# Softmax sums of the first query half from the masked first scores

## The chip, the cores and the metric

The kernel runs on one core of a Trainium2 chip. The metric is the device time of one execution in microseconds. Below, TensorE, VectorE, ScalarE, GpSimd and SyncE are the engines that the profile calls PE (PEld for its weight loads), DVE, ACT, POOL and SP.

## The reference

Two layers over x of shape 4 x 1024 x 512. Layer 0 is a causal softmax attention (16 heads of 32) with a projection, a residual and a layer norm, then a feed-forward part with ternary weights; layer 1 is a linear attention and a second feed-forward part. The change touches only this:

```
q, k, v = (x @ w).reshape(B, S, H, hd).transpose(0, 2, 1, 3)     # each
scores = einsum('bhqd,bhkd->bhqk', q, k) / sqrt(hd)
scores = where(causal, scores, finfo.min)
attn = softmax(scores, axis=-1)
ctx = einsum('bhqk,bhkd->bhqd', attn, v)
```

## The kernel before, in words

Layer 0's attention works in 16 units (`NU`), each a batch element and a group of four heads (`HPG`). A unit has 1024 queries in two halves of 512 (`CH`), c = 0 and c = 1, and 8 blocks of 128 keys.

Scores are computed twice. The first time (`score_entry`, L971) queries lie on partitions; VectorE adds the causal mask and takes the row maximum in one instruction (`reduce_rows`, L191), whose full output goes to a scrap buffer, `junk`. A half has 16 such tiles: `SHORT` for c = 0, with 128, 256, 384 or 512 keys, `LONG` for c = 1, with 640 to 1024 in two PSUM banks. After a half's last tile the maxima are negated and split into a high and a low part (L195, L198), turned by TensorE (`turn`, L202), copied (L1112) and written by two DMAs (`load_max`, L183) as two more rows of the queries. The second time (`scores_T`, L984) keys lie on partitions, and the two more rows subtract the maximum, so that ScalarE only has to take exp (L1080) into `probs`. GpSimd clears the masked corner of diagonal blocks (L871). TensorE multiplies `probs` with v (`with_v`, L1000, into `O_BANK`) and, for the softmax sums, with a block of ones (`with_ones`, L1011, into `SUM_BANK`). At the end of a half ScalarE copies `O_BANK` (`evacuate`, L1072), and VectorE normalizes in four parts: a transpose of the sums (L1142), a reciprocal (L1145), a transpose back (L1148), a multiplication (L1154). SyncE stores the half (L893).

A unit has ten steps (`STEPS`), three for the first half and seven for the second. The order of TensorE's work is written out as a string for each step: `s` is the scores of one head for this step, `e` the next entry of the *next* unit's first scores, `v` and `o` the products with v and with ones of the step *before*. The entries (`ROUND`, 34 of them) are the 16 short tiles with the turned rows of c = 1 at place 5, then the 16 long ones with the turned rows of c = 0 behind the fifth. The steps hold 9, 3, 3, 3, 3, 3, 2, 4, 2 and 2 entries. Scores of both kinds take the PSUM banks 0 to 5 as a ring: TensorE waits for whoever used a bank before. v of step 3 waits for the copy of the first half (`o_read`), since both halves use one `O_BANK`. ScalarE's instructions stand in one order: the exponentials of step n + 1, then, behind step 3 and behind the next step 0, the copy of a half. The last unit has no entries but one.

The first stage (`phase_qkv0`) computes q, k and v; in its last batch it holds the first scores of unit 0 (L399, `ENTRIES`, `PLACES`), one or two of them between outputs, which ScalarE copies (L503, L507).

Elsewhere in the kernel, `L1410` counts with ScalarE's Square and `accum_out`, `L1423` and `L1100` are plain ScalarE copies in SBUF, and `L1995` has a bias that is a column of SBUF.

Of the kernel before, what the change touches and what calls it, by code (L numbers as in the profile page):

```python
# [26 lines left out]
P = 128  # L27
# [5 lines left out]
CH = 512  # L33
# [120 lines left out]
class Scores:  # L154


    kst: object
# [7 lines left out]
    bound: object  # L165

# [18 lines left out]
    def reduce_rows(self, dve, bank, junk, c, tile, g):  # L185
# [8 lines left out]
    def negate_hi(self, dve, c):  # L194
        return dve.tensor_scalar(self.negmax[:, c, 0, :], self.rowmax[:, c, :], -1.0, None, ALU.mult)  # L195

    def negate_lo(self, dve, c):
        return dve.scalar_tensor_tensor(out=self.negmax[:, c, 1, :], in0=self.rowmax[:, c, :], scalar=-1.0,  # L198
                                        in1=f32(self.negmax[:, c, 0, :]), op0=ALU.mult, op1=ALU.subtract)
# [5 lines left out]
def phase_qkv0(nc, program, psum, ident, x_t, wq, wk, wv, q_dram, k_dram, v_dram, ffn_w, first, qk_stored, v_stored):  # L205
# [12 lines left out]
    with Phase(program) as ctx:  # L218
# [37 lines left out]
        rm_done, nm_ready, max_loaded = sem("p1_rm_done"), sem("p1_nm_ready"), sem("p1_max_loaded")  # L256
        x_v = x_t.rearrange("b (k p) (c t) -> b c p k t", p=P, c=2)
# [6 lines left out]
        TURN = PER_UNIT + 5  # L264
# [15 lines left out]
        with nc.Block() as block:  # L280
# [199 lines left out]
            def _(act):  # L480
                act.sem_inc(v_copied, 4)

# [13 lines left out]
                def body(b, last):  # L496
                    for c in range(2):
                        for o in range(OUTS):
# [9 lines left out]
                            if 4 <= o < 4 + KT and not (c and last):  # L508
                                x_hi(b + c, 1 - c, o - 4)
                batches(act, body)  # L510

            @block.vector
            def _(dve):
# [22 lines left out]
                def maximum(k):  # L536
# [9 lines left out]
                    if c == 1:  # L546
                        dve.wait_ge(s_used, k + 1)
                    elif k >= 4 and k % 2 == 0:
                        dve.wait_ge(s_used, k)
                    to = first.junk[:, k % 2, k % 4 // 2 * CH:] if c == 0 else first.junk[:, k % 2, :]  # L550
                    first.reduce_rows(dve, bank_of(k), to, c, tile, g).then_inc(s_used, 1)
                    if (tile, g) == (CT - 1, HPG - 1):
                        dve.wait_ge(s_used, 2 + k + 1)
                        first.negate_hi(dve, c).then_inc(rm_done, 1)
                        dve.wait_ge(rm_done, c + 1)
                        first.negate_lo(dve, c).then_inc(nm_ready, 1)
# [72 lines left out]
def phase_attention(nc, program, psum, ident, q_dram, k_dram, v_dram, o_dram, ffn_w, first, qkv_stored, tern, kept, tmp, after, ahead):  # L629
# [14 lines left out]
    STEPS = [([(0, 0)], "seseeseeeeseevo"), ([(0, 1), (0, 3)], "sesessevo"),  # L644
             ([(0, 2)], "eeesssvos"), ([(1, 0)], "esesssevo"),
# [4 lines left out]
    HALF_ENDS = [3, N_STEPS]  # L650
    ST_PER_UNIT = HPG * N_STEPS
# [14 lines left out]
    with Phase(program, ahead) as ctx:  # L666
# [40 lines left out]
        sum_read = sem("p2_sum_read", 1)  # L707
        rec_step = sem("p2_rec_step")
# [9 lines left out]
        bias_stage = first.causal[:, 0:D]  # L718
# [1888 lines left out]
```

## Time and profile before

| | us |
|---|---|
| median of 3 runs | 2439.05 (2438.56 to 2439.28) |
| profiled execution | 2436.57 |
| its span | 2435.0 |
| TensorE busy | 2372.1 (97%) |
| VectorE busy | 1214.1 (50%) |
| ScalarE busy | 824.4 (34%) |
| GpSimd busy | 862.6 (35%) |

The span runs from the first to the last instruction of the profile; the 1.6 us beside it lie outside. Busy shares are of the whole span, in which the layer-0 attention is one of six stages, and shares of a stage are read from its own slices and windows. TensorE's instructions are pipelined: the start times of its rows tell how long a group took, and the durations of neighbours overlap. ScalarE's overlap too, so a row that merges n instructions has a duration of n - 1 distances and one last instruction.

### The profile page before, as it was taken

The page shows a single profiled execution, that of the slowest core. Times are in us where ns is not written, and L with a number is a line of the kernel's source. Part 1 is how long each engine was busy: PE and PEld are TensorE (multiplying, and loading weights), DVE is VectorE, ACT ScalarE, POOL GpSimd, SP SyncE. Part 2 cuts the span into 40 slices and gives each one's busy share as a digit, 9 for nine tenths or more (in the row PEclk, how much of TensorE's full clock was granted, in tenths as well). Part 3 has the DMA queues.
Part 4 walks back from the last instruction along what each step waited for, and adds up shares of the span by engine and source line. Part 5 has one row for each costly group of instructions (what it writes and reads, how often), then busy time and mean ns, then how long its engine had stood idle before and what let it go on. Part 6 is the DMA issues. An engine that isn't in the chain of part 4 may idle for free. (4 is left out here: it accounts for less than half of the span.)

```text
span 2435.0 us, 39858 instructions
## 1 busy us (share of the span) xinstructions
PE 2372.1 (97%) x12749; PEld 1783.5 (73%) x12749; DVE 1214.1 (50%) x2551; ACT 824.4 (34%) x1392; POOL 862.6 (35%) x1098
## 2 busy tenths in 40 slices
PE   9999999999999999999999996999999999999997
PEld 7887755555555557788888885888888888888886
DVE  4334577777777758422222207776764732222221
ACT  3222355555555543344444431011111222222221
POOL 2000256565665552233333334442425221222112
PEclk9999999999999999999999998999999999999999
DMA  8895354545445328512121104140404242222200
GB/s 285 282 300 183 109 131 111 142 119 124 118 119 137 100 86 295 139 35 52 34 52 34 40 30 160 36 172 21 152 34 153 89 109 53 52 52 52 58 29 35
DMA packets 265860, 262.55 MB, mean 108 GB/s; under 512 B 128051, under 2 KB 161843, under 8 KB 265269
## 3 DMA queue, kind: packets, MB, share of 16 engines
q1 hardware_dynamic: 250148, 218.44, 31.2%
q0 software_dynamic: 6128, 24.21, 3.2%
q10 hardware_dynamic: 9504, 18.88, 2.3%
q8 instruction: 46, 0.75, 0.1%
q14 instruction: 34, 0.27, 0.0%
HBM read 168.68 MB, written 92.27 MB: 107 GB/s over the span
## 5 line engine op out<-in xcount | busy, mean ns | idle before, releaser
L191 DVE CUSTOM_DVE_ANT_0 junk<-psum,causal 128x896 bf16<-128x896 f32 (+7 forms) x512 | 373.3, 751 | 163.2 <-PE psum L971 137.8
L1080 ACT ACTIVATE p_probs<-psum 128x512 f32<-128x512 f32 (+1 forms) x640 | 317.4, 555 | 269.0 <-PE psum L984 264.8
L1607 POOL TENSOR_TENSOR p_h_lo<-p_h,p_h_hi 128x512 fp32r<-128x512 f32 x128 | 164.3, 1284 | 303.5 <-ACT p_h_hi L1630 303.5
L984 PE MATMUL psum<-qst,kst 98*128 98x512 f32 (+3 forms) x768 | 220.8, 367 | 1.8 <-PEq L280 0.9
L871 POOL TENSOR_SCALAR_AFFINE_SELECT p_probs<-p_probs 128x128 f32<-128x128 f32 x512 | 140.7, 297 | 223.3 <-ACT p_probs L1080 221.0
L2394 ACT ACTIVATE p_h<-psum,ffn_b 128x512 f16<-128x512 f32 x128 | 88.0, 688 | 372.5 <-PE psum L1259 357.6
L2370 POOL CAST p_h<-p_h 128x512 fp32r<-128x512 f16 x128 | 85.0, 664 | 364.6 <-ACT p_h L2394 364.1
L971 PE MATMUL psum<-kst,qst 96*128 96x128 f32 (+3 forms) x720 | 207.7, 362 | 0.8 <-ACT p_probs L1080 0.8
L984 PEld LDWEIGHTS psum<-qst,kst 98*128 98x128 f32 x768 | 130.8, 189 | 106.1 <-DVE rowmax L191 42.7
L1656 PE MATMUL psum<-tern,p_h_hi 128*128 128x512 f32 x512 | 199.4, 390 | 2.5 <-POOL p_h_lo L1607 2.5
L1656 PE MATMUL psum<-tern,p_h_lo 128*128 128x512 f32 x512 | 199.3, 389 | 0.0
L1622 ACT ACTIVATE p_h<-psum,ffn_b,alpha 128x512 f32<-128x512 f32 x128 | 99.8, 780 | 260.6 <-PE psum L1259 256.7
L971 PEld LDWEIGHTS psum<-kst,qst 96*128 96x128 f32 x720 | 123.6, 189 | 69.5 <-DVE rowmax L191 42.6
L2474 DVE TENSOR_TENSOR ffn_rows<-psum,p_b 128x512 f16<-128x512 f32 x32 | 19.9, 683 | 280.5 <-PE psum L2418 280.5
L1000 PE MATMUL psum<-p_probs,v 128*32 128x512 f32 (+3 forms) x1536 | 157.0, 496 | 1.9 <-ACT p_probs L1080 1.1
L1011 PE MATMUL psum<-p_probs,p_ones 128*32 128x512 f32 (+3 forms) x1536 | 154.4, 489 | 0.0
L1259 PE MATMUL psum<-ffn_xT,la_w_hi 128*128 128x512 f32 x384 | 149.6, 389 | 1.2 <-PEq L1859 1.2
L2418 PE MATMUL psum<-p_w_hi,p_h 128*128 128x512 f32 x384 | 149.5, 389 | 0.0
L2418 PE MATMUL psum<-p_w_lo,p_h 128*128 128x512 f32 x384 | 149.4, 389 | 0.0
L1259 PE MATMUL psum<-ffn_xT,la_w_lo 128*128 128x512 f32 x384 | 149.4, 389 | 0.0
L1656 PEld LDWEIGHTS psum<-tern,p_h_hi 128*128 128x128 f32 x512 | 96.1, 188 | 23.2 <-issue 1.8
L1656 PEld LDWEIGHTS psum<-tern,p_h_lo 128*128 128x128 f32 x512 | 96.0, 188 | 19.9
(260 smaller groups left out, 4902.5 us busy)
## 6 DMA issues: line engine op xcount, KB each, us to landing
qst<-q_parts SPq DMA_DIRECT2D x96, 256.0 KB, 4.8
kst<-k_parts SPq DMA_DIRECT2D x96, 256.0 KB, 6.8
q_parts<-p_qk_out SPq DMA_DIRECT2D x32, 512.0 KB, 3.7
k_parts<-p_qk_out SPq DMA_DIRECT2D x32, 512.0 KB, 3.4
v_rows<-p_v_out SPq DMA_DIRECT2D x32, 256.0 KB, 4.4
v<-v_rows SPq DMA_DIRECT2D x16, 512.0 KB, 4.1
attention_out<-p_o_out SPq DMA_DIRECT2D x32, 256.0 KB, 2.1
p_x<-in_x SPq DMA_DIRECT2D x8, 1024.0 KB, 6.7
```

What stands on the lines that cost most here:

```text
L191: return dve.tensor_tensor_reduce(view(junk[:, 0:n]), bank, view(self.causal[:, SEQ - n:SEQ]), 1.0, FLOOR, ALU.add, ALU.max, self.rowmax[: ...
L871: pool.affine_select(out=blk, in_=blk, compare_op=ALU.is_ge, fill=0.0, base=0, pattern=[[1, P]], channel_multiplier=-1).then_inc(p_masked, 1)
L971: mm = pe.matmul(psum[:, bank, 0:keys], qst[slot][0:KD, c, g, tile * P:(tile + 1) * P], kst[slot][0:KD, g, k0:k0 + keys], start=True, stop ...
L984: mm = pe.matmul(psum[:, bank, col:col + CH - q0], kst[s][0:KD + 2, g, j * P:(j + 1) * P], qst[s][0:KD + 2, c, g, q0:CH], start=True, stop ...
L1000: mm = pe.matmul(O_BANK[g * HD:(g + 1) * HD, q0:CH], vs[s][:, j, g * HD:(g + 1) * HD], probs[:, n % 2, g, col:col + CH - q0], start=(n == ...
L1011: mm = pe.matmul(SUM_BANK[g * HD:(g + 1) * HD, q0:CH], ones[:, :], probs[:, n % 2, g, col:col + CH - q0], start=(n == half_at), stop=(n + ...
L1080: act.activation(probs[:, n % 2, g, col:CH], psum[:, banks_of(s, "s", st)[0], col:CH], ACT.Exp, scale=SM_SCALE).then_inc(p_ready, 1)
L1259: mm = pe.matmul(bank, lhsT, rhs, start=(n == 0), stop=(n == len(terms) - 1))
L1607: pool.tensor_tensor(h_lo[:, m % 2, :], h[:, m % 2, :], f32(h_hi[:, m % 2, :]), ALU.subtract).then_inc(hl_done, 1)
L1622: H.free(act.activation(h[:, t % 2, :], H.bank(m), ACT.Gelu, bias=b1c[:, t:t + 1], scale=alpha[:, 0:1]), m)
L1656: mm = pe.matmul(Y.bank(m), src[:, t % 2, tok], tern2[:, t, :], start=(t == 0 and part == 0), stop=(t == HT - 1 and part == 1))
L2418: mm = pe.matmul(Y.bank(m), h[:, t % 2, a * P:(a + 1) * P], w(t), start=(t == 0 and part == 0), stop=(t == HT - 1 and part == 1))
```

## The change

The softmax sums of the first half no longer come from products with ones. VectorE's instruction for a short tile now writes the masked scores, times minus the scale, as f32 to one of three slots of `junk`, and takes their minimum. ScalarE then takes exp of the slot in place with the row's extreme as bias and the row sum as accumulated output (`sum_row`), two entries behind (`SUM_BEHIND`), between its exponentials of the unit in work (`work`). After the sixteenth sum it takes the logarithm and exp of its negative (`logarithms`); VectorE corrects the logarithm with these and subtracts it from the maximum (`fold`), behind the fifth long tile (`FOLD`), and only then splits the shift. The probabilities of the first half are so already normalized: the products with ones, and VectorE's normalization, are dropped for it, and ScalarE copies `O_BANK` straight to the output buffer. The strings of steps 1 to 3 lose their `o`. The rows of c = 0 are turned behind the eighth long tile instead of the fifth. VectorE waits for the sum of three tiles before when it reuses a slot. ScalarE's wait for the buffer of probabilities is for the products with v where there are none with ones. The causal mask becomes bf16. In the first stage the 16 sums of unit 0 stand between ScalarE's copies of the last batch, and a preload of the table set natural_log_exp_and_others is issued at its start.

```diff
+        if c == 0:
+            return dve.tensor_tensor_reduce(junk[:, 0:n], bank, self.causal[:, SEQ - n:SEQ], -SM_SCALE, -FLOOR,
+                                            ALU.add, ALU.min, self.rowmax[:, c, col:col + 1])
...
+    def sum_row(self, act, n, tile, g):
+
+        scores, col = self.slot(n)[:, 0:P * (tile + 1)], g * CT + tile
+        return act.activation(scores, scores, ACT.Exp, bias=self.rowmax[:, 0, col:col + 1], scale=-1.0,
+                              accum_out=self.sums[:, 0, col:col + 1])
+
+    def logarithms(self, act, log_done, inverse_done, value):
+
+        act.activation(self.sums[:, 1, :], self.sums[:, 0, :], ACT.Ln).then_inc(log_done, 1)
+        act.wait_ge(log_done, value)
+        act.activation(self.sums[:, 2, :], self.sums[:, 1, :], ACT.Exp, scale=-1.0).then_inc(inverse_done, 1)
...
+        dve.tensor_tensor(self.sums[:, 3, :], self.sums[:, 0, :], self.sums[:, 2, :], ALU.mult).then_inc(ratio_done, 1)
+        dve.wait_ge(ratio_done, value)
+        dve.scalar_tensor_tensor(out=self.sums[:, 2, :], in0=self.sums[:, 3, :], scalar=-1.0, in1=self.sums[:, 1, :],
+                                 op0=ALU.add, op1=ALU.add).then_inc(log_better, 1)
+        dve.wait_ge(log_better, value)
+        dve.scalar_tensor_tensor(out=self.sums[:, 4, :], in0=self.sums[:, 2, :], scalar=-1.0, in1=self.rowmax[:, 0, :],
+                                 op0=ALU.mult, op1=ALU.add).then_inc(folded, 1)
...
-        TURN = PER_UNIT + 5
+        FOLD, TURN = PER_UNIT + 4, PER_UNIT + 8
...
-    STEPS = [([(0, 0)], "seseeseeeeseevo"), ([(0, 1), (0, 3)], "sesessevo"),
-             ([(0, 2)], "eeesssvos"), ([(1, 0)], "esesssevo"),
+    STEPS = [([(0, 0)], "seseeseeeeseevo"), ([(0, 1), (0, 3)], "sesessev"),
+             ([(0, 2)], "eeesssvs"), ([(1, 0)], "esesssev"),
...
+        FOLD, LONG_BEHIND = LONG[4], 8
+        ROUND = SHORT[:BEHIND] + [(0, 1, None, None)] + SHORT[BEHIND:] + LONG[:LONG_BEHIND] + [(1, 0, None, None)] + LONG[LONG_BEHIND:]
...
-                    if n == half_at:
-                        pe.wait_ge(sum_read, 2 * u + blocks_of(n)[0][0] + 1)
+                    if n == HALF_ENDS[0]:
+                        pe.wait_ge(sum_read, u + 1)
...
-                    act.wait_ge(o_normed, 1 + 2 * u + c)
-                    act.activation(o_raw[:, :], O_BANK, ACT.Copy).then_inc(o_read, 1)
+                    if c == 0:
+                        act.wait_ge(o_stored[0], 1 + 16 * u)
+                        act.activation(o_out[:, 0, :], O_BANK, ACT.Copy).then_inc(o_read, 1)
...
+                def row_sum(u, k):
+                    if k < 0 or ROUND[k] not in SHORT:
+                        return
+                    _, _, tile, g = ROUND[k]
+                    n = SHORT.index(ROUND[k])
+                    if n == 0:
+                        act.wait_ge(folded, 1 + u)
+                    act.wait_ge(s_used, S_RING + PER_ROUND * u + k + 1)
+                    first.sum_row(act, n, tile, g).then_inc(sum_done, SUMMED_TO[n + 1] - SUMMED_TO[n])
+                    if n == PER_UNIT - 1:
+                        act.wait_ge(sum_done, PER_ROUND * u + SUMMED_TO[-1])
+                        first.logarithms(act, log_done, inverse_done, 1 + u + 1)
+                        act.sem_inc(sum_done, PER_ROUND - SUMMED_TO[-1])
+
+                def work(u, s, n, end=False):
+
+                    wait_probs(u, n)
+                    head, k = 0, ENTRY_AT[n]
+                    for what in STEPS[n][1]:
+                        if what == "s":
+                            exponential(u, s, n, head)
+                            head += 1
+                        elif what == "e":
+                            if not end:
+                                row_sum(u, k - SUM_BEHIND)
+                            k += 1
...
-                        to = first.junk[:, (n + 2) % 4 // 2, n % 2 * CH:]
-                        alone = n % 2 == 0
+                        to = first.slot(n)
+                        if n >= 3:
+                            dve.wait_ge(sum_done, at + 1)
...
+                    if e == FOLD:
+                        dve.wait_ge(inverse_done, 1 + u + 1)
+                        first.fold(dve, ratio_done, log_better, folded, 1 + u + 1)
+                        dve.wait_ge(folded, 1 + u + 1)
+                        shift(unit, 0)
...
+                           far("junk", [P, 3, SEQ], BF16), far("rowmax", [P, 2, HPG * CT], F32), far("negmax", [P, 2, 2, HPG * CT], F32R),
+                           far("max_rows", [2 * HPG * CT, 2, P], F32), far("causal", [P, SEQ], BF16), far("bound", [P, 2, 3], F32),
+                           far("sums", [P, 5, HPG * CT], F32))
```

## Rows read from the trace of the kernel before

**Rows 1.** the page, 40 slices of the span (60.9 us each), busy tenths.

```profile
ACT  3222355555555543344444431011111222222221
...
PEclk9999999999999999999999998999999999999999
```

**Rows 2.** grouped lines, 285 to 896 us; busy, mean ns, idle before and releasers.

```profile
L191 DVE CUSTOM_DVE_ANT_0 junk<-psum,causal 128x128 bf16<-128x128 f32 (+3 forms) x480 | 349.0, 750 | 143.5 <-PE psum L971 137.8 <-issue 2.8 <-DVE rowmax L191 0.3
...
L1011 PE MATMUL psum<-p_probs,p_ones 128*32 128x512 f32 (+3 forms) x1536 | 154.4, 489 | 0.0
```

**Rows 3.** windows, steps 0-3 and 4-9: length, busy PE, PEld, DVE, ACT, POOL (x instructions), clock.

```profile
554.58:568.17 13.59, 13.52 (x124) 8.23 (x120) 10.79 (x44) 8.41 (x18) 6.19 (x17) 1.00 0.68 169
568.17:593.01 24.84, 24.84 (x175) 12.12 (x171) 18.75 (x36) 12.62 (x25) 16.33 (x24) 1.00 0.40 99
```

**Rows 4.** timeline of TensorE: start, duration, line, tiles, count.

```profile
554.58 0.50 PE L984 MATMUL psum<-qst,kst 98*128 98x512 f32 x1
...
560.11 1.07 PE L1000 MATMUL psum<-p_probs,v 128*32 128x512 f32 x8
...
561.97 0.90 PE L971 MATMUL psum<-kst,qst 96*128 96x384 f32 x3
...
563.16 1.07 PE L1000 MATMUL psum<-p_probs,v 128*32 128x384 f32 x16
...
565.02 0.39 PE L984 MATMUL psum<-qst,kst 98*128 98x256 f32 x1
...
567.17 0.64 PE L1000 MATMUL psum<-p_probs,v 128*32 128x256 f32 x8
...
568.17 0.74 PE L984 MATMUL psum<-qst,kst 98*128 98x512 f32 x2
...
569.36 1.06 PE L1000 MATMUL psum<-p_probs,v 128*32 128x512 f32 x8
570.36 0.56 PE L971 MATMUL psum<-kst,qst 96*128 96x320 f32 x2
...
573.27 1.06 PE L1000 MATMUL psum<-p_probs,v 128*32 128x512 f32 x8
...
593.04 0.51 PE L984 MATMUL psum<-qst,kst 98*128 98x512 f32 x1
```

**Rows 5.** timeline of ScalarE in the same unit.

```profile
555.12 1.58 ACT L1080 ACTIVATE p_probs<-psum 128x512 f32<-128x512 f32 x3 [2.23 <-PE psum L984]
...
558.01 0.60 ACT L1072 ACTIVATE p_o_raw<-psum 128x512 f32<-128x512 f32 x1 [0.32 <-PE psum L1000]
558.76 2.07 ACT L1080 ACTIVATE p_probs<-psum 128x512 f32<-128x512 f32 x4 [0.16 <-PE psum L984]
563.03 0.94 ACT L1080 ACTIVATE p_probs<-psum 128x256 f32<-128x256 f32 x3 [2.20 <-PE psum L984]
```

**Rows 6.** timeline of ScalarE elsewhere.

```profile
895.91 2.18 ACT L1100 ACTIVATE kst<-pieces 128x512 fp32r<-128x512 f32 x4
...
958.95 1.92 ACT L1423 ACTIVATE qst<-p_o 128x2048 fp32r<-128x2048 f32 x1 [9.86 <-PE psum L1259]
960.78 1.90 ACT L1410 ACTIVATE p_squares<-tern 128x2048 f16<-128x2048 f32 x1
962.57 0.19 ACT L1410 ACTIVATION_READ_ACCUMULATOR p_squares<-tern 128x1 f32 x1
962.79 1.92 ACT L1410 ACTIVATE p_squares<-tern 128x2048 f16<-128x2048 f32 x1
...
1498.41 2.42 ACT L1995 ACTIVATE p_qT<-psum,p_bq 128x512 f32<-128x512 f32 x4 [7.28 <-issue]
```

**Rows 7.** grouped lines of VectorE, 285 to 896 us.

```profile
L1154 DVE TENSOR_TENSOR p_o_out<-p_o_raw,p_recip 128x512 f32<-128x512 f32 x31 | 40.8, 1317 | 0.1
```

**Rows 8.** timeline of ScalarE in the first stage.

```profile
222.88 0.60 ACT L503 ACTIVATE p_qk_out<-psum 128x512 fp32r<-128x512 f32 x1 [1.94 <-PE psum L457]
```

**Rows 9.** grouped lines of ScalarE, whole span; one of three such rows.

```profile
L1435 ACT ACT_TABLE_LOAD x1 | 1.3, 1283 | 0.0
```

More of the change, by code:

```diff
@@ L165 @@
     bound: object
+    sums: object
     def load_qk(self, eng, q_dram, k_dram, u, s, c, r, of_q, loaded):
@@ L480, in _, with row_sums @@
             def _(act):
+                act.preload_act_table_set("natural_log_exp_and_others")
                 act.sem_inc(v_copied, 4)
+                def row_sums(entries):
+                    for k in entries:
+                        if k < PER_UNIT:
+                            act.wait_ge(s_used, 2 + k + 1)
+                            first.sum_row(act, k, *ENTRIES[k][1:]).then_inc(sum_done, 1)
+                        if k == PER_UNIT - 1:
+                            act.wait_ge(sum_done, PER_UNIT)
+                            first.logarithms(act, log_done, inverse_done, 1)
                 def x_hi(b, c, k, at_start=False):
@@ L509, in body @@
                                 x_hi(b + c, 1 - c, o - 4)
+                            if last and c == 0:
+                                row_sums(PLACES[0][o])
                 batches(act, body)
@@ L794, in phase_attention @@
         PARTS = 4
-        AFTER = [HALF_ENDS[c] % N_STEPS for c in range(2)]
-        FROM = [ENTRY_AT[n] + entries_in(STEPS[n][1].split("o")[0]) for n in AFTER]
-        TO = [FROM[c] + PARTS - 1 for c in range(2)]
-        assert TO[1] < FROM[0] and turned(1) < FROM[1]
+        FROM = entries_in(STEPS[0][1].split("o")[0])
+        TO = FROM + PARTS - 1
+        assert turned(1) < FROM and TO < PER_ROUND
+        SUM_BEHIND = 2
+        SUMMED_TO = [0] + [ROUND.index(e) + 1 for e in (SHORT + LONG)[3:PER_UNIT + 3]]
         def half(eng, body):
@@ L1085, in _ @@
                     act.wait_ge(stored, value)
-                exponentials(0, 0, 0)
+                work(0, 0, 0)
                 def body(i, last):
@@ L1091, in body @@
                         if n + 1 < len(steps):
-                            exponentials(*steps[n + 1])
+                            work(*steps[n + 1], last and steps[n + 1][1] == 1)
                         if step + 1 in HALF_ENDS:
@@ L1159, in entries, with normalize_between @@
                         maximum(at, banks_of(s, "e", k), ROUND[k], u)
[L1161 removed]
+                def normalize_between(u, around, s, first):
                     for part in range(PARTS):
[L1164 removed]
+                        normalize(u, part)
                         if part < PARTS - 1:
@@ L1192, in body @@
                         if last and s == 1:
-                            for part in range(PARTS):
-                                normalize(u, 0, part)
                             split_projection()
                             for part in range(PARTS):
-                                normalize(u, 1, part)
+                                normalize(u, part)
                             return
-                        entries(u, s, TO[1], FROM[0])
-                        normalize_between(u, 0, u, s, FROM[0])
-                        entries(u, s, TO[0], PER_ROUND)
+                        entries(u, s, TO, PER_ROUND)
                         if last:
```

131 lines of the change are left out of this document (81 added, 50 removed).

## The prediction

> **What bounds the kernel now.** I read the slices of the page first: the attention stage runs from about 285 to 895 us, TensorE at its full granted level, ScalarE at five to six tenths [rows 1]. Second come the grouped lines of that stage: the products with ones cost 154.4 us of TensorE there, beside VectorE's masked maxima with 349.0 us [rows 2]. Third, two stretches of one unit: in steps 0 to 3 (13.59 us) TensorE is busy 13.52, VectorE 10.79 and ScalarE 8.41 us; in steps 4 to 9 (24.84 us) TensorE is busy for all 24.84, ScalarE for 12.62 [rows 3]. A busy TensorE need not be a bound one, so the fourth view is its timeline: one unit's first matmul starts at 554.58, the next one's at 593.04, 38.46 us later, and in between the groups start behind one another with no idle time named [rows 4]. So the attention stage is 16 units of 38.4 us, set by TensorE's own order. ScalarE follows it: its exponentials start 0.54 us after the unit's first matmul and then wait for scores [rows 5]. The question for this change is which engine needs longer in each stretch, not over the stage: the new work on ScalarE lies almost wholly in steps 0 to 3.
>
> **What is removed from TensorE.** With ones behind, v and ones of step 0 take 560.11 to 561.97, 1.86 us, and those of step 1 563.16 to 565.02, 1.86 us; a v group with no ones behind takes 569.36 to 570.36, 1.00 us. That is 0.86 us less, twice. Step 2 (256 columns) takes 1.00 us with ones; in the same proportion 0.46 us go. Together 2.18 us a unit [rows 4]. For 16 units this would be 34.9 us, if TensorE stayed the bound.
>
> **What is added to ScalarE.** Every unit but the last prepares the next one's 16 short tiles, so 15 units have 16 sums each, four of each width 128, 256, 384, 512. The order puts sum n at the second entry behind its own. Counting the letters e of the steps: step 0 has 9 entries and so sums 0 to 5 (entry 5 is the turned rows), step 1 sums 6 to 8, step 2 sums 9 to 11, step 3 sums 12 to 14, step 4 sum 15 and the logarithms. ScalarE works in order, and the copy of the first half's output stands behind step 3, so 15 sums lie ahead of it. TensorE cannot start v of step 3 before that copy (with_v waits for o_read).
>
> The price of one sum. Plain instructions behind one another start 0.49 us apart at 512 columns (558.76: four end after 2.07, the last takes 0.60) and 0.28 at 256 [rows 5]. From SBUF, as here, four of 512 end after 2.18 us, 0.52 apart, and one of 2048 is followed after 1.83 us (958.95 to 960.78) [rows 6]. On the line through these, 128, 256, 384 and 512 columns take 0.19, 0.30, 0.41 and 0.52 us. To this comes the accumulator's read: instructions with one start 2.01 us apart (960.78 to 962.79) at 2048 columns, 0.18 more than the plain one. And the sum has its bias in a column of SBUF: four such of 512 columns end after 2.42 us (last 0.69), 0.58 apart, 0.09 more than 0.49 [rows 6]. So 0.27 on each: 0.46, 0.57, 0.68 and 0.79 us. Fifteen of them: 4 x (0.46 + 0.57 + 0.68) + 3 x 0.79 = 9.21 us, 0.61 each.
>
> ScalarE's demand from its first exponential to the end of the copy: 12 exponentials of 512 at 0.49 and 4 of 256 at 0.28, 7.00 us; the copy of the former unit's second half, 0.75 to the next instruction (558.01 to 558.76) [rows 5]; the sums, 9.21; the copy itself, 0.60. That is 17.56, and with the start at 0.54 the copy ends 18.10 us into the unit. In the kernel before v of step 3 starts at 569.36, 14.78 us into the unit [rows 4]. TensorE alone would be there at 14.78 - 2.18 = 12.6. So ScalarE becomes the bound of steps 0 to 3, and v of step 3 is 3.3 us later than before.
>
> Bounds of this term. Below: if the column's 0.09 lies under the instruction before, 15 x 0.09 = 1.35 less, +2.0. Above: ScalarE's first exponential of a step waits twice, for the probabilities' buffer and the scores; a copy with such a pair behind it is followed after 0.75 instead of 0.49, so up to 0.15 for each of four steps, and 0.1 to reach TensorE: +4.0. I take +3.5, as some of such waits will show on an engine that never idles.
>
> **Whether it is caught up.** From v of step 3 on, TensorE had 593.04 - 569.36 = 23.68 us with no idle time [rows 4], so a delay is kept. ScalarE has 3.91 us until v of step 4 (573.27): four exponentials 1.96, sum 15 with 0.79, and two tiny instructions with waits of their own for the logarithm, some 0.8 us by estimate. 3.55 fits, barely; a few tenths may show and lie in the range. From step 5 on ScalarE is half idle.
>
> **The other parts.** VectorE waits for a sum three tiles back before it reuses a slot, with later maxima and the turned rows queued behind, and TensorE's bank ring behind those. Its 10.79 us of steps 0 to 3 fit in 18, and sum n - 3 precedes in ScalarE's order, so this is ScalarE's pace again and is not counted twice. The half's normalization (two transposes, a reciprocal, a multiplication of 1.3 us) goes from VectorE [rows 7]; TensorE did not wait for it, so nothing is gained. Fold and shift add five operations of 16 columns there, beside it. The reductions read a bf16 mask and write f32: with one f32 source in PSUM I expect the same 750 ns mean; 10% either way, some 0.7 us on the 16 short ones, is covered while ScalarE sets the pace. The rows turned for the first half come three entries later, in step 6, and are needed in the next step 0, over 10 us later. The store waits for the copy instead of VectorE and leaves sooner; SP's later loads move with the unit. In the first stage 16 sums fall between outputs where ScalarE idles 1.94 us [rows 8], two sums (1.0 to 1.4 us) each: nothing. The last unit has no sums and saves up to 2.18 us, but its first steps already wait elsewhere; I take 1.
>
> **Sum.** 15 x 3.5 - 1 = +51.5 us. The profiled execution took 2436.57 us (span 2435.0); with it 2488. The median of the runs is 2.5 us above it: 2490.5, so 2490.
>
> **Rivals.**
> 1. The accumulator and the bias column cost nothing in a stream of short instructions, so that sums run at the plain pitch. For it: VectorE's own accumulator reads hide well. Against: ScalarE's read stands in its rows with time of its own between instructions [rows 6]. Then 15 sums take 5.16 us, v of step 3 starts at 14.05, 0.73 earlier: 15 x 0.73 + 2 = 13 us faster, 2426. It decides from a mean price of 0.61 - 3.3 / 15 = 0.39 us a sum down. Chance 0.12.
> 2. TensorE stays the bound, all 34.9 us come: 2404. That needs 15 sums in 3.7 us, 0.25 each, less than a plain 256 [rows 5], or waits that let TensorE go past them; the ring of six banks and the copy behind step 3 forbid it. Chance 0.05.
> 3. Half-way: part of the 0.27 hides, and the copies overlap better: 0 to +28 us, 2439 to 2467. Chance 0.13, of which 0.05 within 0.2%.
> 4. Two table loads a unit, one for Ln and one back, or waits on own results much longer than counted. In the trace of before a load takes 1.28 us, three in all [rows 9], since Exp and Copy need no change. 2 x 1.28 x 15 = 38 more, 2528 with full effect; partial effects end at 2500 to 2515. The preload added at the start speaks against. Chance 0.10.
> By the Trainium skill, "ScalarE: Activation LUTs", section "Table sets: the hidden batching unit", one set (natural_log_exp_and_others) holds exp and ln, so no load is needed between them; no row of before has an Ln to show it. By that rule rival 4 comes only from the waits; the chance above is already low by the preload alone.
>
> **Chances.** The forecast, ScalarE bound in steps 0 to 3: 0.60, own range 2467 (15 x 2.0 - 2) to 2498 (15 x 4.0 - 1). About 0.2%, 5 us, is what a measurement can tell from no change. Faster: 0.12 + 0.05 = 0.17. Same 0.05. Slower 0.60 + 0.08 + 0.10 = 0.78. The range goes from rival 1 (2426) to a part of rival 4 (2515).
>
> **What would show it.** In the profile after: units of about 42 us; TensorE idle ahead of scores and v groups of steps 0 to 3, released by ScalarE or by VectorE that waited for ScalarE's sums; ScalarE without gaps there, and sums 0.46 to 0.79 us apart; steps 4 to 9 as before; v groups of the first half 1.00 us to the next. Were units at 36.3 us, rival 2 holds; if sums take 0.4 us or less, rival 1; if table loads stand in the attention stage, rival 4.

## The result and the profile after

The changed kernel takes 2490.12 us (median of 4 runs, 2488.42 to 2498.07), the kernel before beside it 2439.16 (4 runs, 2438.56 to 2439.55): ratio 1.0218, interval 1.0205 to 1.0231, 51 us slower. The forecast was 2490. The profiled execution took 2488.42 us, with a span of 2486.7. The total came out as forecast, but two of its steps did not, and they nearly cancel: ScalarE costs less than I put, and the later half of each unit, which I put at nothing, costs as much again.

Line numbers below are those of each run's own kernel. In the changed one L1048 is the first scores, L1061 the second scores, L1077 the products with v, L1087 those with ones, L197 and L199 VectorE's reductions of short and long tiles, L209 the sums, L1164 the exponentials, L1149 and L1152 the copies of the first and second half and L945 GpSimd's mask; in the experiments they move by a few lines.

The page of the changed kernel, engines and three slice rows, answers to [rows 1]:

```profile
PE 2375.3 (96%) x12237; PEld 1770.9 (71%) x12237; DVE 1175.1 (47%) x2535; ACT 955.5 (38%) x1936; POOL 868.6 (35%) x1098
...
PE   9999999999999999999999997999999999999997
...
ACT  3223467676767662444444442010111212222221
...
PEclk9999999999999999999999998999999999999999
```

ScalarE stands at six to seven tenths in the attention stage, not five to six. That average names no bound, for TensorE still has nines there. Grouped lines, 285 to 955 us (busy, mean ns of one, idle before and who ended it), answer to [rows 2]:

```profile
L199 DVE CUSTOM_DVE_ANT_0 junk<-psum,causal 128x640 bf16<-128x640 f32 (+3 forms) x240 | 239.6, 1023 | 166.6 <-PE psum L1048 119.3 <-ACT junk L209 42.4 <-PE psum L242 3.8
...
L1048 PE MATMUL psum<-kst,qst 96*128 96x128 f32 (+3 forms) x720 | 221.1, 375 | 28.4 <-DVE rowmax L199 13.5 <-ACT p_probs L1164 13.3
L1077 PE MATMUL psum<-p_probs,v 128*32 128x512 f32 (+3 forms) x1536 | 157.9, 498 | 18.2 <-POOL p_probs L945 10.8 <-ACT p_o_out L1149 7.3
...
L209 ACT ACTIVATE junk<-junk,rowmax 128x128 f32<-128x128 f32 (+3 forms) x240 | 138.2, 587 | 0.4 <-PE psum L1077 0.4
...
L1087 PE MATMUL psum<-p_probs,p_ones 128*32 128x512 f32 (+3 forms) x1024 | 111.1, 517 | 0.0
L209 ACT ACTIVATION_READ_ACCUMULATOR junk<-junk,rowmax 128x1 f32 x240 | 54.1, 225 | 0.0
```

The ones cost 111.1 us instead of 154.4 [rows 2]: they did go. In their place TensorE idles: 28.4 us before score tiles and 18.2 before v groups, where the kernel before had 0.8 and 1.9. ScalarE is named for 13.3 + 7.3, GpSimd for 10.8 (its masks follow ScalarE's exponentials, so this is ScalarE again), and VectorE's long tiles for 13.5. That last one was not in the forecast.

One unit in two stretches, steps 0 to 3 and 4 to 9 (length; busy PE, PEld, DVE, ACT, POOL; clock; DMA), answers to [rows 3]:

```profile
579.60:594.11 14.51, 12.74 (x91) 7.25 (x87) 10.41 (x42) 13.97 (x44) 6.93 (x17) 1.00 0.64 158
594.11:621.85 27.74, 26.01 (x175) 12.01 (x171) 16.74 (x38) 15.21 (x33) 15.88 (x24) 1.00 0.34 89
```

The first stretch is 0.92 us longer than before, with ScalarE busy 13.97 of 14.51 us; the second 2.90 longer, although ScalarE is busy for little more than half of it. Part of that second figure is steps 0 to 3 still arriving late (the v of step 3 falls in it). TensorE's timeline of this unit (start, duration, line, tiles, [idle before <- releaser]) divides it, and answers to [rows 4] (units come in two lengths, 42.25 and 41.5 us in turn; this is one of the longer):

```profile
579.60 0.50 PE L1061 MATMUL psum<-qst,kst 98*128 98x512 f32 x1
...
585.72 0.44 PE L1048 MATMUL psum<-kst,qst 96*128 96x384 f32 x1 [0.40 <-ACT p_probs L1164]
...
589.31 1.07 PE L1077 MATMUL psum<-p_probs,v 128*32 128x384 f32 x16 [0.65 <-POOL p_probs L945]
...
592.81 0.80 PE L1048 MATMUL psum<-kst,qst 96*128 96x320 f32 x2 [0.54 <-ACT p_probs L1164]
...
596.16 1.06 PE L1077 MATMUL psum<-p_probs,v 128*32 128x512 f32 x8 [0.40 <-ACT p_o_out L1149]
...
602.89 0.62 PE L1048 MATMUL psum<-kst,qst 96*128 96x384 f32 x2 [0.64 <-DVE rowmax L199]
...
610.61 0.47 PE L1048 MATMUL psum<-kst,qst 96*128 96x448 f32 x1 [0.59 <-DVE rowmax L199]
...
621.85 0.50 PE L1061 MATMUL psum<-qst,kst 98*128 98x512 f32 x1
```

The v of step 3 starts 16.56 us into the unit, released by the copy, against 14.78 before: 1.8 us later, not 3.3. From it to the next unit TensorE needs 25.69 us instead of 23.68 [rows 4]: 2.0 more in this unit, with two waits for long tiles in it. ScalarE over the first of these parts, answers to [rows 5]:

```profile
580.14 1.08 ACT L1164 ACTIVATE p_probs<-psum 128x512 f32<-128x512 f32 x2 [2.23 <-PE psum L1061]
581.11 0.40 ACT L209 ACTIVATE junk<-junk,rowmax 128x128 f32<-128x128 f32 x1
581.40 0.20 ACT L209 ACTIVATION_READ_ACCUMULATOR junk<-junk,rowmax 128x1 f32 x1
581.49 0.60 ACT L1164 ACTIVATE p_probs<-psum 128x512 f32<-128x512 f32 x1
...
584.59 0.59 ACT L1152 ACTIVATE p_o_raw<-psum 128x512 f32<-128x512 f32 x1
585.06 0.60 ACT L1164 ACTIVATE p_probs<-psum 128x512 f32<-128x512 f32 x1
...
595.43 0.68 ACT L1149 ACTIVATE p_o_out<-psum 128x512 f32<-128x512 f32 x1
...
597.82 0.22 ACT L214 ACTIVATE sums<-sums 128x16 f32<-128x16 f32 x1
598.07 0.22 ACT L216 ACTIVATE sums<-sums 128x16 f32<-128x16 f32 x1
598.23 1.09 ACT L1164 ACTIVATE p_probs<-psum 128x512 f32<-128x512 f32 x2
```

No idle time is named between 580.14 and the copy. Over the stage, a sum is followed by the next instruction after 0.384, 0.491, 0.598 and 0.706 us (medians of 60 each, from start to start, by width 128 to 512). Fifteen are 4 x (0.384 + 0.491 + 0.598) + 3 x 0.706 = 8.0 us. No table load stands around the logarithm. VectorE in step 5:

```profile
597.96 0.82 DVE L199 CUSTOM_DVE_ANT_0 junk<-psum,causal 128x640 bf16<-128x640 f32 x1 [1.33 <-ACT junk L209]
...
602.75 0.20 DVE L220 TENSOR_TENSOR sums<-sums 128x16 f32<-128x16 f32 x1
602.98 0.17 DVE L222 SCALAR_TENSOR_TENSOR sums<-sums 128x16 f32<-128x16 f32 x1
...
603.61 0.17 DVE L238 SCALAR_TENSOR_TENSOR negmax<-sums,negmax 128x16 fp32r<-128x16 f32 x1
603.86 0.96 DVE L199 CUSTOM_DVE_ANT_0 junk<-psum,causal 128x768 bf16<-128x768 f32 x1
```

The five operations of fold and shift take 1.1 us, from 602.75 to 603.86, and stand between two long tiles. TensorE's wait of 0.64 us at 602.89 above is for the long tile ahead of them, whose reduction ends as they start. What they cost shows a little later; in the unit before this one:

```profile
563.48 0.73 PE L1061 MATMUL psum<-qst,kst 98*128 98x512 f32 x2 [0.43 <-DVE rowmax L199]
```

There TensorE waits for the long tile that stands behind the fold.

The table that the rest goes by: the time from the first matmul of each v group to that of the next, taken from the matmul records of each trace, medians over 14 units in us (mean of even and odd units where they differ; kernels named by their experiments below).

```
                     9>0   0>1   1>2   2>3  | 3>4   4>5   5>6   6>7   7>8   8>9 | unit
before               2.89  3.05  4.01  2.20 | 3.90  5.34  3.56  5.51  3.47  4.51 | 38.43
changed              3.52  3.21  4.04  2.81 | 3.90  6.48  4.04  5.56  3.46  4.84 | 41.86
1 one column         2.89  2.19  3.35  1.77 | 3.90  8.36  4.91  5.55  3.46  4.55 | 40.92
2 no accumulator     3.23  3.09  3.53  2.63 | 3.90  6.75  4.04  5.56  3.46  4.75 | 40.94
3 long tiles to PSUM 3.52  3.21  4.04  2.82 | 3.92  6.56  4.07  5.56  3.47  4.84 | 42.01
4 unused ones        3.52  3.21  4.45  2.82 | 3.90  6.47  4.03  5.55  3.46  4.84 | 42.25
5 fold earlier       3.52  3.21  4.04  2.81 | 3.90  8.85  4.23  5.55  3.46  4.84 | 44.42
6 fold later         3.52  3.21  4.04  2.82 | 3.90  6.47  3.76  5.14  3.46  4.84 | 41.16
7 column, fold later 2.89  2.19  3.35  1.77 | 3.90  6.47  3.76  5.14  3.46  4.55 | 37.48
8 spread             2.76  4.33  3.54  1.65 | 3.83  5.34  3.93  8.18  5.85  4.83 | 44.45
```

The change costs 3.43 us a unit (forecast 3.5): 1.43 in the first four columns and 0.33 in the last, which is ScalarE; 1.67 in columns 4>5 to 6>7, which is something else. Of these 1.67, 4>5 grows by 1.1 us in every unit, but 5>6 only in every second one (4.51 us; 3.57 in the others, as before).

The granted clock differs between these traces. From 300 us to the stage's last v group it was 1.00 throughout in the kernel before, the changed one and experiments 2, 4 and 7. It was at the lower level (0.50, 1.2 GHz) for 3 us in experiment 6, 7 in 3, 41 in 1, 58 in 5 and 61 in 8. In experiment 1 a unit with 6.8 us of it takes 42.0 us, a unit of the same kind without it 39.0. So a microsecond at the lower level costs some 0.44 us (3.0 / 6.8), which makes 18, 25 and 27 us in experiments 1, 5 and 8, by estimate. Their rows of the table hold this too.

### The profile page after: what moved, and what is told of

It is laid out like the page before. It is cut to its first block and busy times, and to the rows that moved or that the text cites. A ratio compares the mean times of both kernels' runs of the same rounds, so it can differ in the third digit from the quotient of the medians.

```text
span 2486.7 us, 39530 instructions
## 1 busy us (share of the span) xinstructions
PE 2375.3 (96%) x12237; PEld 1770.9 (71%) x12237; DVE 1175.1 (47%) x2535; ACT 955.5 (38%) x1936; POOL 868.6 (35%) x1098
## 5 line engine op out<-in xcount | busy, mean ns | idle before, releaser
L1164 ACT ACTIVATE p_probs<-psum 128x512 f32<-128x512 f32 (+1 forms) x640 | 324.4, 567 | 201.0 <-PE psum L1061 199.4
L199 DVE CUSTOM_DVE_ANT_0 junk<-psum,causal 128x640 bf16<-128x640 f32 (+3 forms) x256 | 256.0, 1023 | 177.1 <-PE psum L1048 119.3
L1048 PE MATMUL psum<-kst,qst 96*128 96x128 f32 (+3 forms) x720 | 221.1, 375 | 28.4 <-DVE rowmax L199 13.5
L945 POOL TENSOR_SCALAR_AFFINE_SELECT p_probs<-p_probs 128x128 f32<-128x128 f32 x512 | 148.6, 312 | 269.2 <-ACT p_probs L1164 267.1
L1061 PE MATMUL psum<-qst,kst 98*128 98x512 f32 (+3 forms) x768 | 227.3, 373 | 5.9 <-DVE rowmax L199 3.5
L1061 PEld LDWEIGHTS psum<-qst,kst 98*128 98x128 f32 x768 | 132.9, 190 | 116.7 <-ACT p_probs L1164 43.6
L1048 PEld LDWEIGHTS psum<-kst,qst 96*128 96x128 f32 x720 | 124.3, 190 | 119.3 <-ACT p_probs L1164 51.8
L1077 PE MATMUL psum<-p_probs,v 128*32 128x512 f32 (+3 forms) x1536 | 157.9, 498 | 18.2 <-POOL p_probs L945 10.8
L197 DVE CUSTOM_DVE_ANT_0 junk<-psum,causal 128x128 f32<-128x128 f32 (+3 forms) x256 | 121.5, 486 | 73.8 <-issue 32.4
L209 ACT ACTIVATE junk<-junk,rowmax 128x128 f32<-128x128 f32 (+3 forms) x256 | 147.0, 584 | 0.4 <-PE psum L1077 0.4
```

What stands on the lines that cost most here:

```text
L197: return dve.tensor_tensor_reduce(junk[:, 0:n], bank, self.causal[:, SEQ - n:SEQ], -SM_SCALE, -FLOOR, ALU.add, ALU.min, self.rowmax[:, c, ...
L209: return act.activation(scores, scores, ACT.Exp, bias=self.rowmax[:, 0, col:col + 1], scale=-1.0, accum_out=self.sums[:, 0, col:col + 1])
L945: pool.affine_select(out=blk, in_=blk, compare_op=ALU.is_ge, fill=0.0, base=0, pattern=[[1, P]], channel_multiplier=-1).then_inc(p_masked, 1)
L1048: mm = pe.matmul(psum[:, bank, 0:keys], qst[slot][0:KD, c, g, tile * P:(tile + 1) * P], kst[slot][0:KD, g, k0:k0 + keys], start=True, stop ...
L1061: mm = pe.matmul(psum[:, bank, col:col + CH - q0], kst[s][0:KD + 2, g, j * P:(j + 1) * P], qst[s][0:KD + 2, c, g, q0:CH], start=True, stop ...
L1077: mm = pe.matmul(O_BANK[g * HD:(g + 1) * HD, q0:CH], vs[s][:, j, g * HD:(g + 1) * HD], probs[:, n % 2, g, col:col + CH - q0], start=(n == ...
```

## The experiments

Eight kernels, each run beside the kernel before; its median was 2438.61 beside experiments 1 to 4, 2438.26 beside 5 and 2437.55 beside 6 to 8.

### 1. The sums nearly taken away

```diff
-        return act.activation(scores, scores, ACT.Exp, bias=self.rowmax[:, 0, col:col + 1], scale=-1.0,
-                              accum_out=self.sums[:, 0, col:col + 1])
+        return act.activation(self.sums[:, 0, col:col + 1], scores[:, 0:1], ACT.Exp, scale=-1.0)
```

> The kernel after, but a sum reads one column of its slot instead of 128 to 512, without bias and accumulator; its waits, slots and places stay. (Sums are not computed.) Theory, ScalarE's time in steps 0 to 3 sets the unit: 15 such instructions take some 0.2 us each, 3.0 instead of 8.0, so TensorE's own order is the bound again, units near 36.3 us and the time 2404 to 2412. Rival, the hand-over VectorE to ScalarE and back through three slots sets the pace whatever a sum costs: units stay above 39 us, 2450 or more.

Measured 2473.24 (2469.55 to 2476.11), ratio 1.0141 (1.0124 to 1.0158): neither. In the table steps 0 to 3 are at TensorE's pace (first four columns: 10.20, in the changed kernel 13.58), so that half of the theory holds. What was won there is lost in 4>5 and 5>6. Its timeline, three engines mixed:

```profile
628.51 2.36 POOL L911 TENSOR_TENSOR pieces<-pieces,tern 128x1024 f32<-128x1024 f32 x1 [0.18 <-POOL tern L908]
...
629.17 1.73 DVE L219 TENSOR_TENSOR sums<-sums 128x16 f32<-128x16 f32 x1
...
632.83 1.22 PE L1060 MATMUL psum<-qst,kst 98*128 98x512 f32 x2 [1.91 <-DVE rowmax L199]
...
635.69 1.94 PE L1076 MATMUL psum<-p_probs,v 128*32 128x512 f32 x8
```

and the window right behind the wait, columns as above:

```profile
632.85:639.50 6.65, 6.65 (x24) 2.65 (x25) 1.96 (x5) 2.17 (x4) 0.00 (x0) 0.51 0.34 111
```

The reader is to see two things. VectorE's first fold operation, 16 columns wide, takes 1.73 us instead of 0.20: it ends at 630.90, where GpSimd's product of two tiles in SBUF ends (628.51 + 2.36 = 630.87). Over the stage the fifteen of them have a mean of 1.51 us. And after the wait of 1.91 us TensorE ran at a granted clock of 0.51, its 1.2 GHz level: the v group takes 1.94 us instead of 1.07. By the estimate above this lower level is some 18 us of the run. The Trainium skill has the rule for the first, "SBUF — State Buffer", section "SBUF: two separate sides": VectorE and GpSimd share a pair of ports, held by one of them for a whole instruction, and a VectorE operation with two inputs in SBUF needs it against a GpSimd operation that reads SBUF. This trace agrees. In this kernel the fold falls inside GpSimd's product; in the changed kernel ScalarE makes it late enough to fall into the product's last 0.3 us at most.

### 2. The sums without their accumulator

```diff
-        return act.activation(scores, scores, ACT.Exp, bias=self.rowmax[:, 0, col:col + 1], scale=-1.0,
-                              accum_out=self.sums[:, 0, col:col + 1])
+        return act.activation(scores, scores, ACT.Exp, bias=self.rowmax[:, 0, col:col + 1], scale=-1.0)
```

> The kernel after, but the exponentials of the sums have no accumulated output (256 reads fewer; the sums are a constant). Theory: a sum is dearer than a plain exponential by the accumulator's read, 0.18 us each. Fifteen of them in steps 0 to 3 give back 2.7 us a unit, 40 us in all, and VectorE is less late behind them: 2435 to 2450. Rival, the read hides under the next instruction and the price is the columns': 2485 to 2490.

Measured 2475.55 (2474.15 to 2478.03), ratio 1.0153 (1.0136 to 1.0170), between the theory and its rival. The pitches are now 0.292, 0.400, 0.506 and 0.614 us, 0.092 less each (0.091 at 256). So the read costs 0.092 us in a stream of short instructions, half of the 0.18 that I took from instructions of 2048 columns [rows 6]. Without it they stand within 0.02 of the line of the prediction plus its 0.09 for the bias column (0.28, 0.39, 0.50, 0.61): those terms were right. Per unit 1.10 + 0.09 us are won in the first four columns and 8>9, and 0.27 given back in 4>5. There the fold's first operation comes earlier, towards GpSimd's product:

```profile
L219 DVE TENSOR_TENSOR sums<-sums 128x16 f32<-128x16 f32 x15 | 7.5, 500 | 0.0
```

Its mean is 500 ns against 238 (3.6 us for 15) in the changed kernel, 0.26 more a unit.

### 3. No waits of the long tiles for the sums

```diff
+        out = bank if junk is None else view(junk[:, 0:n])
-        return dve.tensor_tensor_reduce(view(junk[:, 0:n]), bank, ...
+        return dve.tensor_tensor_reduce(out, bank, ...
...
-                        n = LONG.index((1, c, tile, g))
-                        to = first.junk[:, n % 3, :]
-                        if n < 3:
-                            dve.wait_ge(sum_done, at + 1)
-                        elif n % 2 == 1:
-                            dve.wait_ge(s_used, S_RING - 2 + at + 1)
+                        to = None
```

> The kernel after, but the long tiles' full output goes back to their own PSUM banks, so VectorE needs no slot for them and waits for no sum there. Theory: 1.9 us of a unit's 3.4 us loss lie behind v of step 3, and most of it is VectorE, which waits for sums 14 and 15 before long tiles 1 and 2 (1.1 and 1.3 us in the trace after) and is late for TensorE's bank ring in steps 5 to 7: 1.2 to 1.6 us a unit come back, 2466 to 2473. Rival, those late steps come from the fold's chain of five operations or from ScalarE itself: 2485 to 2491. Should PSUM output be slow, the long tiles' mean (1023 ns) shows it.

Measured 2500.80 (2492.95 to 2503.85), ratio 1.0259 (1.0242 to 1.0276): the theory fell. The profiled execution is the fastest of the four, with a mean granted clock of 0.992; the others had 0.985 to 0.988, so part of the median is clock that the table doesn't show. VectorE's 42.4 us of waits for `junk` are gone, and no column of the table is shorter. A named wait of 1.1 to 1.3 us, some tiles ahead of the place that hurts, was slack. The long tiles cost a little more each than with 1023 and 83 ns; the rest of the 0.15 us a unit is not explained:

```profile
L200 DVE CUSTOM_DVE_ANT_0 psum<-psum,causal 128x640 f32<-128x640 f32 (+3 forms) x240 | 243.7, 1043 | 162.8 <-PE psum L1049 158.6 <-PE psum L243 2.9
...
L200 DVE DVE_READ_ACCUMULATOR2_ANT rowmax<- 128x1 f32 x240 | 33.9, 141 | 0.0
```

### 4. The ones put back, unused

```diff
-    STEPS = [([(0, 0)], "seseeseeeeseevo"), ([(0, 1), (0, 3)], "sesessev"),
-             ([(0, 2)], "eeesssvs"), ([(1, 0)], "esesssev"),
+    STEPS = [([(0, 0)], "seseeseeeeseevo"), ([(0, 1), (0, 3)], "sesessevp"),
+             ([(0, 2)], "eeesssvps"), ([(1, 0)], "esesssevp"),
...
+                        elif behind and what == "p":
+                            unused_ones(*behind)
```

> The kernel after with the first half's products with ones put back at their old places, their result unused: TensorE gets its 2.18 us a unit again. Theory: in steps 0 to 3 TensorE waits for ScalarE, 16.6 us against 12.6 of its own, so the products lie in that wait: 2490 to 2500. Rival, TensorE's work still counts in full there: 15 to 16 times 2.18, 2523.

Measured 2495.35 (2495.19 to 2496.63), ratio 1.0234 (1.0217 to 1.0251), as expected. Products that the kernel before paid with 2.18 us a unit cost 0.39 here, all of it in 1>2. So in steps 0 to 3 TensorE is not the bound of the changed kernel, and removing them brought next to nothing.

### 5. The fold one long tile earlier

```diff
-        FOLD, LONG_BEHIND = LONG[4], 8
+        FOLD, LONG_BEHIND = LONG[3], 8
```

> The kernel after with FOLD = LONG[3] instead of LONG[4]: nothing else moves. The e3 run did not give back the loss behind v of step 3, so that part of the theory fell. New theory: it is VectorE's chain of five small operations (1.1 us) put between long tiles 4 and 5, exactly when TensorE's ring asks for their banks; behind long tile 3 VectorE idles 2.3 us, and the chain is free there. v of step 4 to v of step 6 (10.5 us against 8.9 before) comes back to 9.0 to 9.3, 1.2 to 1.5 us a unit: 2467 to 2473. Rival, the delay behind v of step 3 is ScalarE's order or the later turn of the rows: 2487 to 2492.

Measured 2529.29 (2527.48 to 2535.18), ratio 1.0380 (1.0360 to 1.0400): 39 us slower than the changed kernel, where I expected a gain; the rival's 2487 to 2492 did not come either. Its timeline:

```profile
617.83 0.94 DVE L220 TENSOR_TENSOR sums<-sums 128x16 f32<-128x16 f32 x1
...
618.92 2.38 POOL L912 TENSOR_TENSOR more<-more,tern 128x1024 f32<-128x1024 f32 x1 [0.18 <-POOL tern L909]
619.01 2.32 DVE L225 SCALAR_TENSOR_TENSOR sums<-sums,rowmax 128x16 f32<-128x16 f32 x1
...
622.84 0.62 PE L1048 MATMUL psum<-kst,qst 96*128 96x384 f32 x2 [2.21 <-DVE rowmax L199]
```

GpSimd's product (618.92 + 2.38 = 621.30) starts 0.09 us ahead of VectorE's operation, and VectorE's ends at 621.33. The fold's first operation, with 0.94 us, ended in the same way with the operation that GpSimd did before (616.35 to 618.73, a difference of two tiles). A reduction, whose scores are in PSUM, ran inside that one without growing: 0.82 us at 617.09, as at 597.96 above.

Column 4>5 rises by 2.37 us, and the wait is the smaller part of it. In the six units that keep the full clock it is 7.55 us, 1.1 more than in the changed kernel; in every second unit it is 10.1, and there the clock is low:

```profile
577.00:583.80 6.80, 6.28 (x21) 2.75 (x25) 3.47 (x9) 2.02 (x4) 0.55 (x1) 0.50 0.23 77
```

So of the 39 us some 25 are the lower level's, by the estimate under the table.

### 6 and 7. The fold and the turned rows later

```diff
-        FOLD, LONG_BEHIND = LONG[4], 8
+        FOLD, LONG_BEHIND = LONG[7], 11
...
-                        if not end:
+                        if last and not end:
                             load_max(1 - s, 0, PER_ROUND * u + turned(0))
...
                                 load(u + 2, s, c)
+                                if c == 0:
+                                    load_max(1 - s, 0, PER_ROUND * u + turned(0))
```

> The kernel after with the fold behind long tile 7 (was 4), the rows of the first half turned behind long tile 10 (was 7), and on SyncE their load behind the next queries' loads instead of ahead of them. The run with the fold one tile earlier showed why it must not stand in GpSimd's stretch: there two small operations with both sources in SBUF ended only with GpSimd's 1024-column tensor_tensor (0.94 and 2.32 us instead of 0.17), and TensorE stood 2.2 us; scalar_tensor_tensor waits like tensor_tensor, against what I thought. Theory: behind long tile 7 GpSimd is idle and VectorE has 2.3 us to spare, so the loss between v of step 4 and v of step 6 (1.5 us a unit) comes back: 2464 to 2472. Rival, that loss is ScalarE's or VectorE's lateness from steps 0 to 3: 2485 to 2492.

Measured 2479.39 (2477.33 to 2481.15), ratio 1.0168 (1.0151 to 1.0185): 11 us of the changed kernel's loss come back, in 5>6 and 6>7, 0.70 us a unit; both ranges are missed. The wait of 0.59 us at 610.61 above is gone. Column 4>5 does not move, with no fold in step 5 any more; why is told under experiment 7. Experiment 7 is the same with the one-column sums of experiment 1:

> The same fold and turn, and one-column sums. (Sums are not computed.) Theory: neither ScalarE's time, nor the fold's place, nor GpSimd stands in the way, TensorE's own order is the bound, units are 36.3 us and the whole of the 34.9 us of the products with ones shows: 2404 to 2412. Rival, there is a further bound in the hand-over of slots or the ring: 2420 or more.

Measured 2425.07 (2421.29 to 2426.65), ratio 0.9950 (0.9934 to 0.9967). Against experiment 6 this is 54 us (15 x 3.68 would be 55): the sums' whole price on ScalarE, in the first four columns (3.39) and 8>9 (0.29). It also shows what this order of entries gives with sums that cost almost nothing: 12 us of the 35 that TensorE saves. The rival's further bound is there. What stays is in 4>5, the same 6.47 as with sums:

```profile
606.48 0.61 PE L1049 MATMUL psum<-kst,qst 96*128 96x384 f32 x2 [0.64 <-DVE rowmax L199]
```

Step 5 holds entries 21 to 23. Before, one of them was the turned rows (one bank, 0.28 us of TensorE); now all three are long tiles of two banks each, beside four transposed scores, in a ring of six. TensorE fills the ring and waits 0.64 us for VectorE's reduction of the first. The other 0.49 of the 1.13 are, I infer, matmuls: from v of step 4 to v of step 5 there are now five long tiles, where before there were four and the turned rows; 6>7 is 0.37 shorter for it. In the changed kernel this stretch holds four long tiles and the turned rows, as before, and the fold. So its 6.48 and this 6.47 have different causes and don't say that the fold was free there.

Why it must wait for a tile of the same step stands in the kernel. `ring` gives a two-bank tile two neighbouring banks and skips one where the tile would start in the last. Worked through for each order, it skips none with the turned rows at their old place. With them behind the eighth long tile it skips two or four in turn, unit by unit. After that the third long tile of step 5 has the two banks of the first, in all units and in both orders, and TensorE can't write it before the first is reduced. In every second unit of the changed kernel a tile of step 7 has one bank of the tile right before it. That is the wait of 0.59 us at 610.61, which stands before the second of the tile's two matmuls, and it is why 5>6 grows in every second unit. With the turned rows behind the eleventh long tile that pair is gone. So what came back in experiment 6 is not the fold's price alone: the order changed the ring as well. The fold's own price in the changed kernel is what TensorE waits behind it, 0.43 us at 563.48.

### 8. Sums spread over seven steps

```diff
-        ROUND = SHORT[:BEHIND] + [(0, 1, None, None)] + SHORT[BEHIND:] + LONG[:LONG_BEHIND] + ...
+        ORDER = "SSSSS1SSS" "S" "LL" "LSL" "SLS" "SLS" "SLS" "LLLL" "L0L" "LLL"
...
+        FOLD = LONG[9]
```

(S and L are a short and a long tile, 1 and 0 the turned rows of the second and first half; long tiles as in experiment 3, the load of the turned rows as in experiment 6. The entries are also spread otherwise over the steps, and the fold's first operation is a scalar_tensor_tensor.)

> A whole version with all sums: eight short tiles in step 0 and one in step 1 as far as ScalarE has room, the other seven between long tiles in steps 3 to 6, three long tiles moved up; long tiles write back to PSUM; the fold behind long tile 9 in step 7, the turned rows of the first half in step 8, their load behind the next queries' loads on SyncE. Theory: ScalarE's 28 us of work fit under TensorE's 36.3 if no stretch holds more than its share; 9 sums in steps 0 to 3 need 4 us less than 15, so a unit is 37 to 38.5 us and the time 2412 to 2440. Rival, VectorE with three slots and the dense long tiles of steps 7 to 9, or the late turned rows, become the bound: 2445 to 2490.

Measured 2539.43 (2531.96 to 2553.81), ratio 1.0437 (1.0397 to 1.0477): it fell, for three reasons that its timeline names, and some 27 us by the lower level of the clock (estimate under the table).

```profile
609.19 0.85 PE L1055 MATMUL psum<-kst,qst 96*128 96x320 f32 x4 [1.03 <-DMA kst<-k_parts]
...
632.13 1.28 POOL L929 TENSOR_TENSOR more<-more 128x512 f32<-128x512 f32 x1
632.25 1.19 DVE L224 SCALAR_TENSOR_TENSOR sums<-sums 128x16 f32<-128x16 f32 x1
...
635.43 0.28 PE L244 MATMUL psum<-ident,negmax 128*32 128x128 f32 x1 [1.82 <-DVE rowmax L200]
```

Long tiles in step 2 come before their keys are loaded (16.9 us over the stage); the fold in step 7 meets a GpSimd addition of two halves of a tile; and the turning waits behind it and two long tiles, 27.1 us in 15 units, with another 22.3 before second scores that wait for long tiles. One part of it says something useful: with a single long tile in step 5, between two short ones, 4>5 is 5.34, exactly as before the change. This supports the ring as the cause in experiments 6 and 7, beside the kernel's own assignment, but other tiles stand in that stretch too. A kernel with the turned rows back in step 5 and nothing else changed was not run, so the ring's price is not isolated. No version that beats the kernel before and computes the whole was found.

## Why the prediction was right, and where it was not

- **What is removed, 2.18 us a unit.** Right: with the sums nearly gone the first four columns take 10.20 us (experiment 7), against 12.15 - 2.18 = 9.97.
- **Which engine then sets steps 0 to 3.** Right. The copy releases the v of step 3, ScalarE has no gap, and 2.18 us of useless products cost only 0.39 (experiment 4).
- **The price of one sum.** Over-sized by 1.2 us in fifteen: 8.0 instead of 9.21. The mis-sized term is the accumulator's read, 0.092 and not 0.18 us. The same bias sits in the copy of the former unit's second half, followed after 0.47 and not 0.75 us (584.59 to 585.06), since the 0.75 held a wait. The demand from first exponential to the copy's end was 15.97 us (580.14 to 596.11), forecast 17.56; the difference is 1.2 + 0.3 and 0.1 over. Rival 1 said that accumulator and bias cost nothing; they cost 0.09 each.
- **The v of step 3.** 1.8 us later in the unit shown, below my own lower bound of 2.0: the bound let go of the bias column, which was real, and held on to the whole of the accumulator's 0.18, half of which was not.
- **Whether it is caught up.** "Kept" was right for 3>4 (3.90 in both). It then grew by 1.67 us a unit, which I had not seen.
- **"Needed over 10 us later", the turned rows.** This step failed. I asked only when the turned rows are needed and not what their place holds: three long tiles now stand in step 5 against a ring of six banks. In the changed kernel the two waits that follow from the ring's banks are 0.64 us in every unit (602.89) and 0.59 us in every second one (610.61). With the fold out of the way 0.95 us a unit stay in 4>5 to 6>7 (experiment 6), and the kernel's `ring` and experiment 8 support the ring as their cause.
- **Fold and shift "beside it".** This failed too. They are 1.1 us between two long tiles on an engine that TensorE's ring waits for, and TensorE waits 0.43 us behind them (563.48). With the fold and the turned rows both later 0.70 us a unit come back (experiment 6), part of it by the ring's other banks; a fold moved alone to a place without GpSimd was not run. The Trainium skill's rule on the shared ports spoke against it and I did not weigh it; in the changed kernel it costs little (mean 238 ns against 175 of the undisturbed operations), in experiments 1, 5 and 8 a great deal. The trace of the kernel before had the sign of it. The 1.3 us of the normalization's multiplication [rows 7] are a mean of 0.69 us in the second half and of 1.9 in the first, where GpSimd is at work on tiles in SBUF until 574.62:

```profile
572.23 2.39 POOL L835 TENSOR_TENSOR tern<-more 128x1024 f32 x1 [0.28 <-POOL more L832]
573.31 1.86 DVE L1154 TENSOR_TENSOR p_o_out<-p_o_raw,p_recip 128x512 f32<-128x512 f32 x1
...
599.86 0.69 DVE L1154 TENSOR_TENSOR p_o_out<-p_o_raw,p_recip 128x512 f32<-128x512 f32 x1
```

- **The sum.** 1.43 + 0.33 + 1.67 = 3.43 us a unit; forecast 3.5. That this fits is the sum of an error of some +1.7 and one of -1.67: luck, and no merit of the terms. Nor are the 51.7 us between the two spans simply 15 such units. The table's 14 units make 47.5, the first unit 2.2, its time up to the first v group 2.6, what lies behind the stage 0.9, and the last unit gives back 1.4 (forecast 1). At the stage's start the changed kernel had a granted clock of 0.67 for 10.2 us (285.90 to 296.10), the kernel before 1.00; why is open.
- **Rivals.** 1 and 3 are out: the price of a sum is 0.53 us, above the 0.39 from which rival 1 decides, and the loss is above 28 us. 2 would not have come even with sums that cost almost nothing: 2425 in experiment 7, not 2404. 4 is out: no table load.

## What to carry to other kernels

Work moved from the engine that bounds to one with average idle time must fit into the stretch where it lands; here ScalarE needed 16.0 us up to the copy, where TensorE alone would have been there after some 12.6. When an entry of a written-out order moves, count what the step that it left and the step that it entered now hold of every shared resource, not only when its result is needed. Place small VectorE operations with two SBUF sources away from GpSimd's work on tiles in SBUF: sixteen columns can take as long as a thousand. And before a slower run is laid to a wait, read the granted clock of every unit: in experiment 5 the lower level cost more than the wait.

## What the runs showed of the hardware that I had not expected

- VectorE operations with two sources in SBUF (128x16, 0.17 us alone) took 1.73, 2.32 and 1.19 us until GpSimd's operation on tiles in SBUF ended, to within 0.03 us (experiments 1, 5 and 8). An operation of 128x16 thus gave TensorE a wait of 1.9 to 2.2 us.
- ScalarE's accumulator read adds 0.092 us to a short instruction in a stream, although its own row shows 0.19 to 0.31: most of the row overlaps.
- VectorE's accumulator read takes 141 ns behind a reduction that writes to PSUM, 83 (19.8 us for 240) behind one that writes bf16 to SBUF, and 81 (19.5 for 240) behind the short tiles', which write f32 to SBUF: the place makes the difference, not the type.
- After a wait of 1.91 us TensorE was granted 1.2 GHz for 6.65 us (0.51) in experiment 1. In the unit of experiment 5 a wait of 2.21 us was followed by 1.00, in the unit before it (577.00 to 583.80) one of 2.26 by 0.50. So a wait of this length doesn't always do it; what decides was not tried. Experiments 1 and 5 spent 41 and 58 us of the stage so.
